# State-space decoder layer: thirteen products by C on VectorE instead of eleven, a large delta at the chunk beginnings instead of cleared columns, one copy moved to ScalarE and one store to SyncE

## What is computed

```python
dA = jnp.exp(jnp.einsum('bld,dn->bldn', delta, A))          # A = -exp(A_log), so dA < 1
dBu = jnp.einsum('bld,bln,bld->bldn', delta, Bm, u)
def step(carry, inp):
    a, bu, c = inp
    carry = a * carry + bu
    y = jnp.einsum('bkdn,bkn->bkd', carry, c)
    return (carry, y)
init = jnp.zeros((Bsz, nc, d_inner, n_state), x.dtype)       # a new start at each chunk of 64 tokens
```

## Time and profile before

| | before |
|---|---|
| median of 3 runs | 2763.23 us (2756.91 to 2768.07) |
| the profiled execution | 2763.72 us, span 2761.9 us |
| mixers, scans of 32 batches | to about 2180 us of the span |
| TensorE / VectorE / ScalarE / GpSimd busy, whole span | 88% / 77% / 65% / 75% |
| the same, from 1000 to 2000 us | 88.9% / 92.8% / 80.3% / 96.6% |
| granted TensorE clock, from 1000 to 2000 us | 0.98 |

### The profile page before, as it was taken

One profiled execution on the slowest core, in us unless ns is written; L12 is line 12 of the kernel. 1 busy time (PEld: TensorE's weight loads), 2 busy tenths in 40 slices (PEclk: granted clock), 3 DMA queues, 4 the chain that ended last, 5 costly groups with the idle time before them and its releaser, 6 DMA issues. The chain is left out here.

```text
span 2761.9 us, 49852 instructions
## 1 busy us (share of the span) xinstructions
PE 2428.5 (88%) x14854; PEld 1665.1 (60%) x14854; DVE 2137.8 (77%) x3587; ACT 1802.4 (65%) x3972; POOL 2072.0 (75%) x967
## 2 busy tenths in 40 slices
PE   6678889888888898988888888989887879999997
PEld 4456666666666666666666666666665545555554
DVE  3788999999999999999999999999999732322333
ACT  3567888787888888877878787878887541111111
POOL 4999999999999999999999999999999500000000
PEclk8788999999999999999999999999999879999999
DMA  5365566666666666666666666666665342342221
GB/s 152 112 143 151 159 166 167 162 160 159 162 167 164 173 161 172 169 162 163 163 164 162 164 161 172 172 162 167 172 162 155 93 119 70 104 132 81 79 79 31
DMA packets 270171, 399.68 MB, mean 145 GB/s; under 512 B 115441, under 2 KB 190449, under 8 KB 265810
## 3 DMA queue, kind: packets, MB, share of 16 engines
q1 hardware_dynamic: 254546, 384.95, 52.8%
q10 hardware_dynamic: 15360, 11.55, 1.5%
HBM read 300.89 MB, written 94.37 MB: 143 GB/s over the span
## 5 line engine op out<-in xcount | busy, mean ns | idle before, releaser
L516 POOL TENSOR_TENSOR arena<-arena 128x1024 f32<-128x1024 f32 x512 | 1208.0, 2363 | 86.5 <-DMA arena<-w_dram 63.6
L615 ACT ACTIVATE dA_ps<-arena,a_neg 128x252 f32<-128x252 f32 x2048 | 868.8, 461 | 319.4 <-DVE dA_ps L819 172.6
L796 DVE TENSOR_TENSOR_SCAN arena<-dA_ps,arena 128x512 f32<-128x512 f32 x672 | 803.1, 1208 | 72.5 <-ACT dA_ps L615 34.5
L526 POOL TENSOR_TENSOR arena<-arena 128x1024 f32<-128x1024 f32 (+1 forms) x416 | 808.0, 1942 | 18.1 <-DVE arena L796 16.9
L796 DVE TENSOR_TENSOR_SCAN dA_ps<-dA_ps,arena 128x512 f32<-128x512 f32 x352 | 416.2, 1205 | 5.3 <-POOL arena L516 3.7
L925 PE MATMUL a_ps<-xT,w_conv 128*128 128x256 f32 x1536 | 365.5, 388 | 0.0
L867 DVE TENSOR_REDUCE mx<-s_ps 128x2 f32<-128x512 f32 x497 | 333.5, 671 | 22.8 <-PE s_ps L925 22.8
L925 PEld LDWEIGHTS a_ps<-xT,w_conv 128*128 128x128 f32 x1536 | 285.7, 192 | 53.4 <-issue 16.1
L925 PE MATMUL y_ps<-arena,sel 128*32 128x256 f32 x4096 | 257.1, 393 | 53.8 <-DVE m_rows L873 27.8
L673 ACT ACTIVATE probs<-st_ps 128x512 f32<-128x512 f32 x493 | 285.2, 578 | 25.7 <-PE st_ps L925 19.7
L925 PE MATMUL s_ps<-k_st,q_st 96*128 96x256 f32 x994 | 259.3, 343 | 41.8 <-DVE mx L867 28.5
(11 more groups left out here) (118 smaller groups left out, 3288.5 us busy)
## 6 DMA issues: line engine op xcount, KB each, us to landing
arena<-delta_dram SPq DMA_DIRECT2D x512, 128.0 KB, 2.8
arena<-w_dram SPq DMA_DIRECT2D x512, 128.0 KB, 3.2
arena<-bc_dram SPq DMA_DIRECT2D x128, 256.0 KB, 4.4
q_st<-q_parts_dram SPq DMA_DIRECT2D x512, 64.0 KB
k_st<-k_parts_dram SPq DMA_DIRECT2D x512, 64.0 KB
w_dram<-u SPq DMA_DIRECT2D x32, 512.0 KB, 2.8
delta_dram<-delta SPq DMA_DIRECT2D x32, 512.0 KB, 3.8
k_parts_dram<-parts SPq DMA_DIRECT2D x32, 512.0 KB, 3.8
```

The source lines that it names most:

```text
L516: pool.tensor_tensor(dBu[:, n % NB], w_r[:, n // RP % 2, t % RP].unsqueeze(1).to_broadcast([P, QS, L]), bc_r[:, b.par, 0], ALU.mult).then_ ...
L526: pool.tensor_tensor(h[:, n % NH, states], h[:, n % NH, states], bc_r[:, b.par, 1, states], ALU.mult).then_inc(s_hC, 1)
L615: last = nc.scalar.activation(dA[n % NDA][:, q, :, 1:], delta_r[:, n // (2 * RP) % 2, t % RP].rearrange("p (c t) -> p c t", t=CH)[:, :, 1: ...
L796: nc.vector.tensor_tensor_scan(dst, decays, dBu[:, n % NB, 2 * half:2 * half + 2].rearrange("p q t -> p (q t)"), 0.0, ALU.mult, ALU.add).t ...
```

## The change

- `delta` gets the value 1e20 at the four chunk beginnings after w has been computed from it (a `memset` of 128x16 on GpSimd, right behind `w_piece`). exp(1e20 * A) is then zero there, and the decays of a half are written whole, 256 columns an instruction instead of 252. `delta_store` waits for this memset (`s_cut`) instead of for `softplus`.
- `clear_starts` and the three memsets of the banks at the program's start go. ScalarE waits for `s_hC_v` (the product on VectorE) or `s_scan`; GpSimd waits for the scan alone.
- Halves (3, 1) and (12, 1) join `HC_DVE`: 13 halves. GpSimd multiplies 128x512 instead of 128x1024 in tiles 3 and 12.
- `x1T_evac` moves from VectorE (slot 9, second in its order) to ScalarE (slot 8, behind `softmax_exp`).
- `store_x2`, four DMAs a batch, moves from ScalarE's queue (slot 5) to SyncE's (slot 6, behind `load_stack`).

```diff
-HC_DVE = [(1, 0), (1, 1), (4, 1), (5, 0), (5, 1), (6, 1), (8, 0), (9, 1), (10, 0), (10, 1), (14, 1)]
+HC_DVE = [(1, 0), (1, 1), (3, 1), (4, 1), (5, 0), (5, 1), (6, 1), (8, 0), (9, 1), (10, 0), (10, 1), (12, 1), (14, 1)]
             def delta_store(b):
-                wait_all(sp, (s_delta, 2, b, 2), *[(s, 128, b.back(2), 128) for s in s_rep])
+                wait_all(sp, (s_cut, 1, b, 1), *[(s, 128, b.back(2), 128) for s in s_rep])
...
             def w_piece(b):
...
+                pool.wait_ge(s_w, b.value(1, 1))
+                starts = delta[:].rearrange("p k (c t) -> p k c t", t=CH)[:, :, :, 0:1]
+                nc.gpsimd.memset(starts, CUT).then_inc(s_cut, 1)
...
                     if n >= NDA:
-                        act.wait_ge(s_scan[(n - NDA) % 2], (n - NDA) // 2 + 1)
+                        b_was, rest = divmod(n - NDA, 2 * NU)
+                        was = divmod(rest, 2)
+                        if was in HC_DVE:
+                            act.wait_ge(s_hC_v, len(HC_DVE) * b_was + HC_DVE.index(was) + 1)
+                        else:
+                            act.wait_ge(s_scan[was[1]], NU * b_was + was[0] + 1)
                     for q in range(2):
                         last = nc.scalar.activation(
-                            dA[n % NDA][:, q, :, 1:],
-                            delta_r[:, n // (2 * RP) % 2, t % RP].rearrange("p (c t) -> p c t", t=CH)[:, :, 1:],
-                            ACT.Exp, scale=a_neg[:, t, 2 * half + q:2 * half + q + 1])
+                            dA[n % NDA][:, q], delta_r[:, n // (2 * RP) % 2, t % RP], ACT.Exp, scale=a_neg[:, t, 2 * half + q:2 * half + q + 1])
...
-                (O_N2 + 3, store_x2),
+                (O_X1T, x1T_evac),
...
-            def clear_starts(t, half):
-
-                def piece(b):
-                    state = dA[(2 * b.value(NU, t) + half) % NDA]
-                    dve.wait_ge(s_hC_v, b.value(len(HC_DVE), HC_DVE.index((t, half)) + 1))
-                    nc.vector.memset(state[:, :, :, 0:1], 0.0).then_inc(s_scan[half], 1)
-                return piece
...
-                (O_X1T + 1, x1T_evac),
```

More of the change, by code:

```diff
@@ L35 @@
 EPS = 1e-5
+CUT = 1e20
 CT = 32
@@ L262, in bank @@
             return ctx.enter_context(nc.psum_tensor(name, shape, F32))
-        dA = [bank(f"dA_ps{i}", [P, 2, NCH, CH]) for i in range(NDA)]
+        dA = [bank(f"dA_ps{i}", [P, 2, L]) for i in range(NDA)]
         y_ps = bank("y_ps", [P, L + P])
@@ L456, in load_columns, with store_x2 @@
                     shared.load_columns(sp, 0, ET - P, ET - EC)
+            def store_x2(b):
+                rows = x2_dram.rearrange("(a e n r) d -> n e r a d", a=TT, e=P // EC, r=EC)
+                rows = rows[bass.ds(b.c, 1)].rearrange("n e r a d -> (n e) r a d")
+                wait_all(sp, (s_x2, TT, b, TT))
+                for q in range(X2_DMAS):
+                    sp.dma_start(rows[q], xt[EC * q:EC * (q + 1), b.c % NX]).then_inc(s_x2_st[b.par], 16)
             def store_x2T(b):
@@ L653, in high, with x1T_evac @@
                 return piece
+            def x1T_evac(b):
+                act.wait_ge(s_x1T_mm, b.value(1, 1))
+                if b.back(3):
+                    act.wait_ge(s_of_mm, b.back(3).value(TT, TT))
+                nc.scalar.activation(x1T[:], a_ps[:], ACT.Copy).then_inc(s_x1T, 1)
             def bc_store(b):
@@ L761, in _ @@
             nc.vector.memset(eps, EPS).then_inc(s_const_v, 1)
-            for i in range(NDA):
-                nc.vector.memset(dA[i][:], 0.0).then_inc(s_const_v, 1)
             dve.wait_ge(s_bias_ld, 16 * len(bias_parts))
@@ L788, in piece @@
                     dve.wait_ge(s_dBu, n + 1)
-                    decays = dA[(2 * n + half) % NDA][:].rearrange("p q c t -> p (q c t)")
+                    decays = dA[(2 * n + half) % NDA][:].rearrange("p q t -> p (q t)")
                     dst = h[:, n % NH, 2 * half:2 * half + 2].rearrange("p q t -> p (q t)")
@@ L797, in piece @@
                         dst, decays, dBu[:, n % NB, 2 * half:2 * half + 2].rearrange("p q t -> p (q t)"),
-                        0.0, ALU.mult, ALU.add).then_inc(s_scan_v if (t, half) in HC_DVE else s_scan[half], 1)
+                        0.0, ALU.mult, ALU.add).then_inc(s_scan[half], 1)
                 return piece
@@ L805, in piece @@
                     state = dA[(2 * n + half) % NDA]
-                    dve.wait_ge(s_scan_v, b.value(len(HC_DVE), HC_DVE.index((t, half)) + 1))
+                    dve.wait_ge(s_scan[half], n + 1)
                     if n >= NH:
@@ L895, in head_norm @@
                 return piece
-            def x1T_evac(b):
-                dve.wait_ge(s_x1T_mm, b.value(1, 1))
-                if b.back(3):
-                    dve.wait_ge(s_of_mm, b.back(3).value(TT, TT))
-                nc.vector.tensor_copy(x1T[:], a_ps[:]).then_inc(s_x1T, 1)
             run_steps([
@@ L914, in _ @@
                 *[(O_SCAN + 4 * m + 6, gating(m)) for m in range(ND)],
-                *[(O_SCAN + t, clear_starts(t, half)) for t, half in HC_DVE],
                 (O_Q + 1, low(s_q_hi, s_q_lo)),
```

32 lines of the change are left out of this document (14 added, 18 removed).

## The result

The changed kernel takes 2774.09 us (median of 7 runs, 2767.48 to 2781.03), the kernel before 2756.91 in the same session (7 runs, 2752.49 to 2768.07). The ratio is 1.0058, with an interval from 1.0038 to 1.0078. That is about 16 us slower. The time lies in the predicted range, 6 us above the forecast, but on the other side of the 0.5% line that the prediction drew between "no change" and "slower" (the interval holds that line). The 6 us make the forecast look better than it was: it starts from the 2763.72 us of one execution, 7 us above the median of before here. As a difference it said +4.5 us, and the measured one is +16. In a second session the same kernel gave 2782.0 us and 1.0078 (1.0063 to 1.0093).

The account below looks back on a forecast made before the run. The prediction took a chain of three legs (ScalarE, VectorE, TensorE) as the bound. Its terms, -0.51 + 0.48 + 0.04 + 0.34 - 0.03 - 0.17, gave +0.15 us a period, times 30 +4.5: 2768 us, range 2737 to 2799.

Parts of the forecast that it names:

- What bounds the kernel: Three legs close a 66.74 us period: ScalarE slots 8-11 (16.31), VectorE 11-0 (15.57), TensorE 0-8 (34.01); only edits there count.
- GpSimd as the bound: Rival: GpSimd, 96.6% busy, sets the period, and 1.9 us less work there gives 2707 us; chance 0.10.
- Banks given back earlier: Slot 7: release 1.2 us sooner ends TensorE's 0.37 us wait for probs; ScalarE's copy of conv's result comes 0.51 us earlier.
- The copy of x1T: On ScalarE's leg, ahead of the table load: costs 0.48 us a period; taking it off VectorE gains 0.
- the four columns: Four more columns in each exp on ScalarE's leg: cost 0.04 us a period, ends 0 and 0.1.
- The slow rival: Slot 8: the copy is too much for ScalarE, whose leg starts no sooner; +0.82 to +0.9 a period, 2790 us, chance 0.25.
- The product of (12, 1): VectorE's leg, slot 13: 0.59 us less 0.25 for a wait for TensorE it fills, so +0.34 a period.
- The memsets: Removing 11 from VectorE saves 0.02 us each; one lies on its leg, so -0.03 a period, ends 0 and -0.6.
- GpSimd's share: Two halves fewer on GpSimd, which is on no leg; TensorE's waits for it go, -0.17 us a period.
- (3, 1): Product in slot 4, before a VectorE wait of 1.24 us for TensorE: cost 0, without this cover 0.59 us.
- the x2 store: Four issues move from ScalarE in slot 5 to SyncE in slot 6, neither on a leg: 0.
- delta's store: On SyncE's queue behind w's store, followed by a load that waits 3.7 us a period: cost 0, uncovered 0.3 us.

Follow-up runs that it names:

- no_12: The changed kernel without half (12, 1) in VectorE's list, so 12 halves there: 2754.4 us, 0.9987 of the kernel before.
- fill: The changed kernel with TensorE's transposed score products of heads 4 and 7 issued four times instead of once: 2763.6 us, 1.0016 of the kernel before.
- late_back: The changed kernel with each bank given back only after VectorE's memset of its chunk beginnings, as before: 2802.8 us, 1.0155 of the kernel before.
- no_3: The changed kernel without half (3, 1) in VectorE's list: 2777.6 us, 1.0060 of the kernel before.
- x2_act: The changed kernel with the store of x2 issued by ScalarE again, in slot 5: 2783.7 us (1.0098 of the kernel before), in a second session 2779.5 us (1.0068).
- before_fill: The kernel before with the transposed score products of heads 4 and 7 issued three times instead of once: 2760.3 us, 1.0004 of the kernel before.

## Why the prediction was right and wrong

**What bounds the kernel: right.** Each edit showed up on the leg on which it lies: the copy in ScalarE's, (12, 1) in VectorE's, the release in TensorE's, (3, 1) and x2's store in none. Where another leg moved too, it was by a wait behind the edit or by the place of the half-rate stretches. GpSimd, the busiest engine, lost 4% of its work, its waits for w went from 26.7 to 48.3 us, and the period grew, which refutes GpSimd as the bound. no_12 gives it one half back and is faster.

**Banks given back earlier: right in kind, low by half on TensorE's leg.** TensorE's leg without a stretch fell by 1.19 us, where the forecast had 0.51 + 0.17. One part that it did not see is slot 3. In the kernel before, VectorE's release there holds ScalarE, and so probs and the transposed scores ahead of conv, as it does in slot 7:

```profile
1056.04 0.48 ACT L615 ACTIVATE dA_ps<-arena,a_neg 128x252 f32<-128x252 f32 x1 [1.30 <-DVE dA_ps L819]
...
1056.85 0.57 ACT L673 ACTIVATE probs<-st_ps 128x512 f32<-128x512 f32 x1
```

The conv product of that slot starts at 1057.88 - 1045.06 = 12.82 us into the leg before, and at 12.52 after: 0.30. From there to the last conv it is 18.25 before and 17.66 after: 0.59, not 0.37. Most of the difference lies at the wait itself: from the product ahead of it to the one behind it, it was 75.82 - 74.86 = 0.96 us, and after it is 75.49 - 75.06 = 0.43, since products that do not wait overlap in the records.

```profile
1074.86 0.59 PE L925 MATMUL s_ps<-k_st,q_st 96*128 96x256 f32 x2
```

With ScalarE's earlier copy, 0.15, this period gains 1.04. The other 0.15 of the 1.19 fits TensorE's wait for GpSimd, which went from 4.6 us to 0.8, 0.14 a period, where 0.17 was forecast.

**What is late next: missed.** The prediction followed the gain to ScalarE's copy and stopped there. Right behind it ScalarE waits for VectorE's scan of (7, 0) (0.29 us in the row at 1012.88, 0.42 between the starts), and its leg is 0.44 longer without the copy being counted.

**The copy of x1T, the four columns: right.** 0.49 measured for the copy, 0.48 forecast; what is left of the leg for the columns is 0.02, where 0.04 was forecast. The wait at L873 in slot 9 grew from 1.15 to 2.14 us, where 1.7 or more was asked. The slow rival, that ScalarE would begin its leg no sooner than now, did not come true: without a stretch TensorE's leg ends 1.19 us sooner. Its +0.82 us a period was nearer to the measured 0.67 than the forecast's +0.15 was, but for another reason.

**The product of (12, 1): its own price right by luck, its effect on TensorE missed.** VectorE's leg grew by 0.37, where 0.34 was forecast, and lost 0.46 again in no_12. The forecast was 0.59 for the product less 0.25 for the wait that it fills. Both terms were too small: the leg grows by 0.74 (15.57 to 16.31) where TensorE has no stretch in it, and by 0.09 (16.22 to 16.31) where it has one, which is in 18 of 27 periods and not in half of them. The prediction read that 0.54 us wait as one for TensorE and did not ask why it is there in some periods only: it is the half-rate clock, seen in the kernel before. Not in the sum was who waits for the row maximum behind it: TensorE, 1.36 us at 1036.92:

```profile
1036.92 0.47 PE L920 MATMUL s_ps<-k_st,q_st 96*128 96x256 f32 x2 [1.36 <-DVE mx L870]
```

That wait ends nothing by itself. It counts through the clock: +0.57 us a period, without which the period would have grown by the forecast's size (0.10 for 0.15). no_12 and fill, two edits on different engines, each take all of it away.

**The memsets, GpSimd's share, (3, 1), the x2 store: right.** late_back shows some 0.03 us for a memset, where 0.02 was forecast; no_3 and x2_act show no gain or loss. That delta's store now waits for the memset was undone in no run by itself; in the traces it is issued 0.54 us behind w's store before and 0.52 after, so it is not later.

The forecast of +0.15 a period thus had a gain too small by 0.5, a new wait of 0.42 not seen, and a clock term of 0.57 not seen; that the errors partly cancel, and that the range is wide, is why the time fell into it. What stays open is why the half-rate stretches fall where they do. They are in both kernels; the runs show what moves them off and onto TensorE's leg, not the rule by which they come.

## What to carry to other kernels

When a period closes through several engines, put an added operation in the leg in which its engine waits: a product of one half cost 0.46 us in slot 13 and nothing in slot 9. A gain on one leg is worth only what the next engine can take up, so follow it one instruction further than the edit. On TensorE look at the granted clock by leg, not as a mean: an operation that makes TensorE wait where that is harmless can put a half-rate stretch where it is not.

## What the runs showed of the hardware

- The mean granted clock hardly moves (from 1000 to 2000 us 0.97 after, 0.98 before), while the place of the half-rate stretches decides 1.4 us in each period that has one on TensorE's leg: 34.42 us against 32.97 for the same 225 records. On VectorE's leg in the kernel before one costs 0.65 us. Among the runs of the kernel after, the time goes roughly with the mean clock (2770.6 us at 0.956, 2774.1 at 0.952, 2777.6 at 0.948, but 2781.0 at 0.949). Between kernels it does not: no_12 has 0.947 to 0.954, the kernel after 0.948 to 0.956, and no_12 is some 20 us faster.
- More work made the kernel faster: three more rounds of the score products of two heads a batch took 10 us off (fill), with no half-rate stretch left on TensorE's leg. Where 1 leg of 27 had such a stretch, two more rounds did nothing (before_fill).
- Small memsets of 128x8 in PSUM between VectorE's other operations cost little: two of them made VectorE's leg 16.38 us instead of 16.31.
